# Graph network layers on one core: edges per node counted in the preparation, by ranks in the sorted destinations, and the preparation on tiles of 128 partitions

## The reference, cut to what matters

```python
def mesh_conv(x, src, dst, ea, w1, b1, g, bt, w2, b2):
    m = jnp.concatenate([x[dst], x[src], ea], axis=-1) @ w1 + b1
    m = jax.nn.silu(group_norm(m, g, bt))
    m = m @ w2 + b2
    n = x.shape[0]
    out = jax.ops.segment_sum(m, dst, num_segments=n)
    cnt = jax.ops.segment_sum(jnp.ones((dst.shape[0],), m.dtype), dst, num_segments=n)
    return out / jnp.clip(cnt, 1.0)[:, None]
# block 0: h = mesh_conv(...); norm, silu, + time embedding
#          h = mesh_conv(...) again; norm, silu, + x
#          attention over edges (8 heads, softmax per destination), output layer, norm
# block 1: graph attention (4 heads) over the same edges, with 128 edge features
```

## Time and profile before

| | us |
|---|---|
| median of 3 runs | 15801.92 (15791.97 to 15820.28) |
| span of the profiled execution | 12412.9 |
| median less span | 3389.0 |
| TensorE busy | 10184.1 (82% of the span) |
| VectorE busy | 6784.3 (55%) |
| GpSimd busy | 6565.9 (53%) |
| ScalarE busy | 4227.0 (34%) |

### The profile page before, as it was taken

One profiled execution on the slowest core, in us unless ns is written; L12 is line 12 of the kernel. 1 busy time (PEld: TensorE's weight loads), 2 busy tenths in 40 slices (PEclk: granted clock), 3 DMA queues, 4 the chain that ended last, 5 costly groups with the idle time before them and its releaser, 6 DMA issues. The chain is left out here.

```text
span 12412.9 us, 238807 instructions
## 1 busy us (share of the span) xinstructions
PE 10184.1 (82%) x52788; PEld 7837.8 (63%) x52788; DVE 6784.3 (55%) x13638; ACT 4227.0 (34%) x19321; POOL 6565.9 (53%) x6535
## 2 busy tenths in 40 slices
PE   0018999999999949999999569999996489999994
PEld 0015666666666637777777457777775378888882
DVE  0024555555555447777777546666665545555555
ACT  0003434433343404444344113333332045555552
POOL 0005444444444317777677237777774077777770
PEclk9996666666666658988898669999998589999996
DMA  1013222222222214444444246666663255555652
GB/s 17 14 48 88 83 82 83 82 82 82 82 84 81 65 58 118 123 121 121 116 121 119 72 118 178 180 178 178 180 178 106 57 130 134 136 136 134 134 135 74
DMA packets 1697918, 1336.67 MB, mean 108 GB/s; under 512 B 595131, under 2 KB 1473914, under 8 KB 1695443
## 3 DMA queue, kind: packets, MB, share of 16 engines
q1 hardware_dynamic: 1462376, 792.32, 23.6%
q0 software_dynamic: 234784, 537.91, 16.7%
HBM read 1255.24 MB, written 74.14 MB: 107 GB/s over the span
## 5 line engine op out<-in xcount | busy, mean ns | idle before, releaser
L452 POOL DMA_INDIRECT conv_gath<-b,conv_idx x3232 | 3262.3, 1009 | 3529.4 <-issue 1893.1
L830 POOL DMA_INDIRECT gat_gath<-g,gat_idx x1616 | 1606.2, 994 | 941.6 <-issue 495.5
L830 POOL DMA_INDIRECT attn_gath<-kv,attn_idx x1616 | 1642.8, 1017 | 847.0 <-issue 517.7
L476 PEld LDWEIGHTS conv_z<-conv_win,conv_hotT 128*128 128x128 f32 x6464 | 1226.0, 222 | 934.1 <-issue 705.0
L478 PE MATMUL conv_z<-wc,conv_ea 5*128 5x128 f32 x6464 | 1799.4, 363 | 0.0
L476 PE MATMUL conv_z<-conv_win,conv_hotT 128*128 128x128 f32 x6464 | 1719.6, 353 | 0.0
L594 DVE TENSOR_REDUCE conv_var<-conv_sq 128x32 f32<-128x512 f32 x808 | 551.7, 683 | 1891.1 <-ACT conv_sq L524 1891.0
L478 PEld LDWEIGHTS conv_z<-wc,conv_ea 5*128 5x128 f32 x6464 | 1100.8, 212 | 470.7 <-issue 173.1
L493 PE MATMUL conv_sums<-conv_hot,conv_m 128*128 128x128 f32 x6464 | 1319.2, 372 | 8.3 <-ACT conv_m L556 7.8
L493 PEld LDWEIGHTS conv_sums<-conv_hot,conv_m 128*128 128x128 f32 x6464 | 1138.8, 267 | 201.6 <-issue 167.5
L469 PE MATMUL conv_z<-conv_gath,ident 128*128 128x512 f32 x1616 | 1173.7, 818 | 58.8 <-DMA conv_gath<-b,conv_idx 58.7
(11 more groups left out here) (338 smaller groups left out, 17743.5 us busy)
## 6 DMA issues: line engine op xcount, KB each, us to landing
conv_win<-a SPq DMA_DIRECT2D x3232, 64.0 KB
conv_places<-places SPq DMA_DIRECT2D x202, 512.0 KB
attn_win<-q SPq DMA_DIRECT2D x1616, 64.0 KB
gat_xeT<-in_xeT SPq DMA_DIRECT2D x404, 256.0 KB
conv_gath<-b,conv_idx POOLq DMA_INDIRECT x3232
attn_places<-places SPq DMA_DIRECT2D x101, 512.0 KB
gat_places<-places SPq DMA_DIRECT2D x404, 128.0 KB
attn_gath<-kv,attn_idx POOLq DMA_INDIRECT x1616
```

The lines of the kernel that those rows point to most:

```text
L452: pool.indirect_dma_start(gath[:, b.c * BQ + k, t, :], None, b_table, bass.IndirectOffsetOnAxis(ap=idx[:, b.c, k * QT + t:k * QT + t + 1], ...
L476: nc.tensor.matmul(zt, hotT[:, s6, t * P:(t + 1) * P], win[:, s4, t, :], start=False, stop=False, skip_group_check=True)
L830: pool.indirect_dma_start(gath[:, b.c * BQ + k, t, :], None, table, bass.IndirectOffsetOnAxis(ap=idx[:, b.c, k * QT + t:k * QT + t + 1], a ...
```

## The change

1. The counts go out of `conv_edges`: `hot_b`, `counts`, the matmul with ones and the copies. `sums` has two buffers in both layers. The fold of layer 1 and the node stage "conv1" lose their part of it.
2. The preparation makes the counts. For each node it finds the number of edges whose destination is lower (its rank): first among the 101 first destinations of the batches (a comparison and a sum on VectorE), then among the 16 first destinations of the tiles of that batch, then among the 128 destinations of that tile. Between these, POOL gathers the rows that are needed, 49 indirect DMAs each time (one for each 128 nodes). Two small matmuls with a shift matrix subtract the rank of each node from that of the next.
3. The preparation works on 128 partitions: `cols` is now one table of [128, 2, 1616], `places` [128, 1664] and `mask` [1664, 129], each stored by one DMA; the mask's rows are no longer held eight times but are repeated when they are loaded. The loads of weights are shared between SP's and ScalarE's queues, and those of the edges come first, with a semaphore of their own.
4. The loads of `idx`, `cols`, `n0` and `mask` in the edge stages read from these new layouts.

The names `BT`, `BE` and `NB` of the batches are now `TB`, `EB` and `NBATCH`. The diff, cut:

```diff
-BT = 16
-BQ = BT // QT
-QE, BE = QT * P, BT * P
-NB = -(-E // BE)
-T = NB * BT
+TB = 16
+BQ = TB // QT
+QE, EB = QT * P, TB * P
+NBATCH = -(-E // EB)
+T = NBATCH * TB
 EP = T * P
-FR = -(-NP // NB)
+NB, BT, BE = 1, T, EP
+FR = -(-NP // NBATCH)
 RB = 3
-BODY = (NB - 2) // RB
-assert NBLK % GB == 0 and NGRP % 2 == 1 and BODY * RB + 2 == NB
+BODY = (NBATCH - 2) // RB
+assert NBLK % GB == 0 and NGRP % 2 == 1 and BODY * RB + 2 == NBATCH
 TC = -(-T // P)
 TP = TC * P
+TQ = TP // P
...
+        dst_c = st.sb("dst_c", [P, T], I32)
+        prev_c = st.sb("prev_c", [P, T], I32)
+        n0_all = st.sb("n0_all", [P, T], I32)
+        rel_c = st.sb("rel_c", [P, 2, T])
+
+        dst_q = st.sb("dst_q", [P, TQ * P], I32)
+        n0_q = st.sb("n0_q", [P, TQ], I32)
+        rel_q = st.sb("rel_q", [P, TQ * P], BF16)
+        mask = st.sb("mask", [P, TQ, P + 1])
...
+        below = st.sb("below", [P, NBLK, P])
+        n0_rows = st.sb("n0_rows", [P, NBLK, TB], I32)
+        dst_rows = st.sb("dst_rows", [P, NBLK, P], I32)
...
+        dst_pt = w["dst_b"].rearrange("o (p t) -> (o p) t", p=P)
+        FULL = (T // TQ) * P // P
+        edge_loads = [(n0_all[:, :], w["n0_p"][:, 0:T].to_broadcast([P, T])),
+                      (n0_q[:, :], w["n0_p"].rearrange("o (q t) -> (o q) t", t=TQ)),
+                      (dst_c[:, :], dst_pt), (prev_c[16:P, :], dst_pt[15:P - 1, :]),
+                      (prev_c[0:1, :], dst_pt[0:1, :]), (prev_c[1:16, :], dst_pt[0:15, :]),
+                      (dst_q[0:112, :], w["dst_r"][0, 0:112 * TQ * P].rearrange("(q e) -> q e", q=112)),
+                      (dst_q[112:FULL, :], w["dst_r"][0, 112 * TQ * P:FULL * TQ * P].rearrange("(q e) -> q e", q=FULL - 112))]
...
+            sp.wait_ge(padded, 1)
+            for dst, src in edge_loads:
+                sp.dma_start(dst, src).then_inc(edges_loaded, 16)
+            for dst, src in loads[0::2]:
...
-            sp.wait_ge(dve_made, 1)
-            sp.dma_start(D["cols"].rearrange("b p (a t) -> b a p t", a=2)[:, 0, :, :],
-                         rel_c[:, 0, :].rearrange("b (p t) -> b p t", t=BT)).then_inc(stored, 16)
-            sp.dma_start(D["cols"].rearrange("b p (a t) -> b a p t", a=2)[:, 1, :, :],
-                         rel_c[:, 1, :].rearrange("b (p t) -> b p t", t=BT)).then_inc(stored, 16)
-            sp.dma_start(D["places"], rel_h[:, :]).then_inc(stored, 16)
-            m = D["mask"].rearrange("(b t h) e -> b t h e", t=BT, h=NS)
-            for h in range(NS):
-                sp.dma_start(m[:, :, h, :], mask[:, :, :]).then_inc(stored, 16)
-            sp.wait_ge(stored, 16 * (4 + 3 + NS))
+            sp.wait_ge(cols_made, 1)
+            sp.dma_start(D["cols"], rel_c[:, :, :]).then_inc(stored, 16)
+            sp.wait_ge(places_made, 1)
+            sp.dma_start(D["places"], rel_q[:, :]).then_inc(stored, 16)
+            sp.wait_ge(mask_made, 1)
+            sp.dma_start(D["mask"].rearrange("(q t) e -> q t e", t=TQ), mask[:, :, :]).then_inc(stored, 16)
+            sp.wait_ge(stored, 16 * 7)
...
+            pool.wait_ge(batch_found, 1)
+            for b in range(NBLK):
+                pool.indirect_dma_start(n0_rows[:, b, :], None, w["n0_b"].rearrange("o (k t) -> (o k) t", t=TB),
+                                        bass.IndirectOffsetOnAxis(ap=batch_i[:, b:b + 1], axis=0)).then_inc(n0_gathered, 16)
+            pool.wait_ge(tile_found, 1)
+            for b in range(NBLK):
+                pool.indirect_dma_start(dst_rows[:, b, :], None, w["dst_r"].rearrange("o (t e) -> (o t) e", e=P),
+                                        bass.IndirectOffsetOnAxis(ap=tile_i[:, b:b + 1], axis=0)).then_inc(dst_gathered, 16)
+            pool.wait_ge(dst_gathered, NBLK * 16)
...
+            for dst, src in loads[1::2]:
+                act.dma_start(dst, src).then_inc(loaded, 16)
...
+            pe.wait_ge(ranked, 1)
+            nc.tensor.matmul(p_n[:, 0:2 * NBLK], shift[:, :], tile[:, :, 0:NBLK], start=True, stop=False)
+            nc.tensor.matmul(p_n[:, 0:2 * NBLK], corner[:, :], tile[:, :, 1:NBLK + 1], start=False, stop=True)\
+              .then_inc(degree_ready, 1)
...
+            nc.vector.memset(dst_q[:, :], N).then_inc(padded, 1)
...
+            dve.wait_ge(edges_loaded, EDGE_LOADS)
+            link(nc.vector.tensor_copy(n0_f[:, :], n0_all[:, :].rearrange("p (k t) -> p k t", t=TB)[:, :, 0]))
+            link(nc.vector.tensor_tensor(below[:, :, 0:NBATCH], bc(n0_f[:, :].unsqueeze(1), wide),
+                                         bc(node[:, :].unsqueeze(2), wide), ALU.is_lt))
+            link(nc.vector.tensor_reduce(batch[:, :], below[:, :, 0:NBATCH], AX.X, ALU.add))
+            link(nc.vector.tensor_scalar(batch[:, :], batch[:, :], -1.0, 0.0, ALU.add, ALU.max))
+            link(nc.vector.tensor_copy(batch_i[:, :], batch[:, :]))
+            dve.sem_inc(batch_found, 1)
+
+
+            link(nc.vector.tensor_tensor(rel_c[:, 0, :], dst_c[:, :], n0_all[:, :], ALU.subtract))
+            link(nc.vector.tensor_tensor(rel_c[:, 1, :], dst_c[:, :], prev_c[:, :], ALU.not_equal))
+            link(nc.vector.memset(rel_c[0:1, 1, :], 1.0))
+            dve.sem_inc(cols_made, 1)
+            rel_t = rel_q[:, :].rearrange("q (t e) -> q t e", e=P)
+            link(nc.vector.tensor_tensor(rel_t, dst_q[:, :].rearrange("q (t e) -> q t e", e=P),
+                                         bc(n0_q[:, :].unsqueeze(2), [P, TQ, P]), ALU.subtract))
+            dve.sem_inc(places_made, 1)
             link(nc.vector.memset(mask[:, :, :], -BIG))
             link(nc.vector.tensor_tensor(mask[:, :, 1:P], rel_t[:, :, 1:P], rel_t[:, :, 0:P - 1], ALU.not_equal))
             link(nc.vector.tensor_scalar(mask[:, :, 1:P], mask[:, :, 1:P], -BIG, None, ALU.mult))
-            dve.sem_inc(dve_made, 1)
-
+            dve.sem_inc(mask_made, 1)
...
+            dve.wait_ge(n0_gathered, NBLK * 16)
+            wide = [P, NBLK, TB]
+            link(nc.vector.tensor_tensor(below[:, :, 0:TB], n0_rows[:, :, :], bc(node[:, :].unsqueeze(2), wide), ALU.is_lt))
+            link(nc.vector.tensor_reduce(tile[:, 0, 0:NBLK], below[:, :, 0:TB], AX.X, ALU.add))
+            link(nc.vector.scalar_tensor_tensor(tile[:, 0, 0:NBLK], batch[:, :], float(TB), tile[:, 0, 0:NBLK], ALU.mult, ALU.add))
+            link(nc.vector.tensor_scalar(tile[:, 0, 0:NBLK], tile[:, 0, 0:NBLK], -1.0, 0.0, ALU.add, ALU.max))
+            link(nc.vector.tensor_copy(tile_i[:, :], tile[:, 0, 0:NBLK]))
+            dve.sem_inc(tile_found, 1)
+
+
+            dve.wait_ge(dst_gathered, NBLK * 16)
+            wide = [P, NBLK, P]
+            link(nc.vector.tensor_tensor(below[:, :, :], dst_rows[:, :, :], bc(node[:, :].unsqueeze(2), wide), ALU.is_lt))
+            link(nc.vector.tensor_reduce(tile[:, 1, 0:NBLK], below[:, :, :], AX.X, ALU.add))
+            dve.sem_inc(ranked, 1)
+
+
+            dve.wait_ge(degree_ready, 1)
+            link(nc.vector.tensor_copy(degree[:, :], p_n[:, NBLK:2 * NBLK]))
+            link(nc.vector.scalar_tensor_tensor(degree[:, :], p_n[:, 0:NBLK], float(P), degree[:, :], ALU.mult, ALU.add))
+            link(nc.vector.tensor_scalar(cnt[:, 0, :], degree[:, :], 1.0, None, ALU.max))
+            link(nc.vector.reciprocal(cnt[:, 0, :], cnt[:, 0, :]))
+            link(nc.vector.tensor_scalar(cnt[:, 1, :], degree[:, :], 0.0, 1.0, ALU.max, ALU.min))
...
+    return D["places"].rearrange("q e -> (q e)")[bass.ds(e, n)].unsqueeze(0).to_broadcast([P, n])
...
+    ZQ, SQ = 6, 2
...
-                for dst, src in ((idx[:, b.c, :], w["src_b"][bass.ds(b.i, 1), :, :].rearrange("a p t -> (a p) t")),
-                                 (places[:, b.c, :], D["places"][bass.ds(b.i, 1), :].to_broadcast([P, BE])),
-                                 (cols[:, b.c, :], D["cols"][bass.ds(b.i, 1), :, :].rearrange("a p t -> (a p) t")),
-                                 (ea[:, b.c, :], w["ea"][:, bass.ds(b.i * BE, BE)]),
-                                 (n0[:, b.c, :], w["n0_b"][bass.ds(b.i, 1), :])):
+                for dst, src in ((idx[:, b.c, :], w["src_b"][0, :, bass.ds(b.i * TB, TB)]),
+                                 (places[:, b.c, :], places_of(D, b.i * EB, EB)),
+                                 (cols[:, b.c, :].rearrange("p (a t) -> p a t", a=2), D["cols"][:, :, bass.ds(b.i * TB, TB)]),
+                                 (ea[:, b.c, :], w["ea"][:, bass.ds(b.i * EB, EB)]),
+                                 (n0[:, b.c, :], w["n0_b"][:, bass.ds(b.i * TB, TB)])):
...
-                if l == 1:
-                    done(pe, counts_freed, g)
-                    done(pe, hot_b_ready, g + 1)
-                    nc.tensor.matmul(counts[0:1, :], C["ones_b"][:, :], hot_b[:, k % 2, :], start=True, stop=True)\
-                      .then_inc(counts_ready, 1)
...
-                outs = [(count, first_count, counts[0:1, :], counts_ready, counts_copied, counts_freed)] if l == 1 else []
-                outs.append((acc, first, sums[so][:, :], sums_ready, sums_copied, sums_freed))
```

(35 more changed lines are left out.)

200 lines of the change are left out of this document (98 added, 102 removed).

## The result

| | us | range |
|---|---|---|
| before | 15797.19 | 15791.97 to 15820.28, 4 runs |
| after | 14713.01 | 14705.99 to 14714.28, 4 runs |
| ratio | 0.9302 | 95% interval 0.9286 to 0.9319 |

The change makes the kernel 7.0% faster, 1084 us. 14112 us (10.7%) were forecast, and the range ended at 14500 us, so size and range were wrong and the sign was right. The profiled execution of the changed kernel took 14714.28 us and has a span of 14712.5 us: nothing lies outside of the span. The 3389 us of the kernel before therefore needed another explanation, and the first experiment looks for it.

The account below looks back on a forecast made before the run. TensorE, busy 82% of the 12412.9 us span, was taken as the bound, with the preparation waiting for DMAs. Gains of 1051 + 626 + 5 + 8 = 1690 us took 15802 to 14112 us; range 13600 to 14500 us.

Parts of the forecast that it names:

- The 3389 us: Timed median 15801.92 less profiled span 12412.9 us; the forecast supposed that this rest outside the span stays.
- layer 1's 1051 us: Convolution layer 1 falls from 3399.3 to layer 2's 2348.0 us, as its program becomes that of layer 2.
- the path through the clock: Layer 1: some 640 of TensorE's 853 us busy-time fall come from remaining matmuls running at a higher clock.
- Rival A: Layer 1 keeps its clock and gains some 420 us instead of 1051; time 14743 us; chance 7%.
- the direct part: Layer 1: TensorE loses 211 us of count matmuls and 205 us of idle time before them, some 420 us.
- The mark that I set for A: Layer 1 at 2950 us with a clock of 0.66 would show that it keeps its clock.
- The copies of counts: Layer 1: ScalarE's 412 us of copies lie in the chain ending TensorE's idle time; not counted a second time.
- Rival C: The 3389 us are slower execution of the same work; gain grows by 1.27 to 2150 us, time 13650; chance 15%.
- The preparation: First stage ends at about 196 us instead of 822.5, a gain of 626 us; ends 150 and 330 us.
- Rival D: Preparation's gathers queue at 5.33 us each, 549 us for 98; preparation 600 us, time 14520 us; chance 4%.
- Small parts: Fold of layer 1 gains 5 us, node stage "conv1" 8 us (ends 0 and 16).
- The sum: 1051 + 626 + 5 + 8 = 1690 us off span and median: span 10723 us, time 14112 us.

Follow-up runs that it names:

- the first experiment: The kernel before, unchanged, profiled a second time: 15685.92 us, ratio 1.001, profiled span 15686.8 us.
- e11: The changed kernel, unedited, on a chip where the kernel before took 12508.35 us: 10795.61 us, ratio 0.8639.
- e1: The kernel before, unchanged, run for a second profile: 15685.92 us against 15666.93 us, ratio 1.001.
- e2: The kernel before without counts (reciprocals set to one, division left out), with two buffers of sums in both layers, old preparation and layouts: 15163.95 us, ratio 0.9687.
- e5: The kernel before without counts, with one buffer of sums in both layers: 13096.88 us against 12500.67 us, ratio 1.0484.
- e10: The changed kernel with one buffer of sums instead of two in both convolution layers: 15362.57 us, ratio 0.9699 to the kernel before.
- e6: The kernel before without ScalarE's copies of the counts, cast and count matmul kept: 12353.54 us, ratio 0.9889.
- e3: The changed kernel with `cols` and `idx` stored and read batch by batch as before: 14572.59 us, ratio 0.9309 to the kernel before.
- e4: The changed kernel with all loads of the preparation on SP's queue, none on ScalarE's: 14592.83 us, ratio 0.9322 to the kernel before.

## Why the prediction was wrong, by its steps

**The steps that failed: layer 1's 1051 us taken over to the timed executions, and with it the supposition that the 3389 us stay.** As a statement on the quick trace, the difference of two stages, it was right: e11 takes 1013 us off layer 1 (3399.3 - 2386.1), and the span of 10758.5 us is within 0.4% of the forecast 10723. With it the path through the clock was given too much: TensorE's busy time falls by 812 us between before and e11 (3169 to 2358), near the 853 us that the prediction has, but by 336 us between e1 and the result (3234 to 2898). The time to be forecast was of executions in which layer 2 itself takes 3283 us (e1). There the gain of layer 1 is 508 us (e2 against e1) or 459 us (the result against e1). The excess over the quick kind, supposed to stay, grew from 3274 us before to 3954 us after (14712.5 - 10758.5), in layer 1 above all: from 396 to 950 us. The stage was slow before through its own single buffer; once that is gone it is as slow as layer 2 there, for a reason that stays open.

**Rival A came out by its number, and only in part by its mechanism.** It had 7%: the layer keeps its clock and gives back the direct part only, 420 us, time 14743 us. Measured were 14713 us, a clock of 0.65 before and 0.69 after, and 459 to 508 us. But two of its terms were not what they seemed. The 205 us of idle time were put down to the counts, and in e5 and e10 they stand there without counts (193 and 307 us). And with the counts out and one buffer, TensorE is busy as long as in e1 (3235 us in e10, 3234 in e1): the 211 us of count matmuls came back as slower matmuls at a clock of 0.60. The second buffer then took off 351 us of busy time. That the sum of the two steps lies near 420 us is luck. The mark that I set for A, 2950 us, is missed because it was counted from the quick 3399. The mistake is in the weighing: "layer 2 runs high after equal starts" was read from an execution that was not one of those timed.

**The copies of counts.** The prediction has them in the chain that ends the idle time before the count matmul. The row itself names "issue" for 186 of the 205 us, and e6 took the copies away and gained 56 us. What made the other matmuls slow was the single buffer of sums (e5), a part of the change that the prediction has as a detail of the counting.

**Rival C had the right premise and the wrong arithmetic.** The 3389 us were slower execution of the same work. But the gain does not grow by 1.27 with the time; it shrinks, since the preparation takes 822 us on either kind of chip (DMAs at 16 GB/s) and layer 1 was slow already. That the missing time could be slower execution deserved more than multiplying all by one factor: stage by stage it must lie where the clock was high, in layer 2 too, and then layer 1 cannot come down to 2348 us.

**The preparation: right.** Forecast 196 us, measured 182.8; -640 us instead of -626. The edge loads ended at 20.3 us instead of 28. The gathers took 1051 ns each in the first round and 946 in the second, 49 x 105 ns = 5.1 us more, where 5 was taken for VectorE beside them. The excess lies in four gathers of 1.40 to 2.65 us at 32 to 44 us, while VectorE makes the tables; no run takes VectorE away. The largest operations took 5.3 and 6.7 us as computed. The stores are hidden. The busy shares of the DMA engines and what they moved in the stage, in 40 slices of 4.6 us, show it:

```profile
DMA  3999952066611111111111011111211111110000
GB/s 99 343 253 217 174 105 56 2 227 250 183 6 8 7 6 7 7 6 7 7 6 6 14 50 50 57 49 51 57 46 55 57 43 57 57 43 14 0 0 0
```

The three slices of 227, 250 and 183 GB/s at 37 to 50 us are the stores of `cols`, `places` and `mask`, in some 14 us where 28 had been estimated, and 184 at 16 GB/s. The stores of before, of `cols` and then of `mask`:

```profile
105.00:256.00 151.00, 2.48 (x11) 2.17 (x11) 10.38 (x41) 0.00 (x0) 0.00 (x0) 1.00 0.12 5
408.00:820.00 412.00, 0.00 (x0) 0.00 (x0) 0.00 (x0) 0.00 (x0) 0.00 (x0) 1.00 0.07 17
```

The Trainium skill (DMA: Bandwidth & Descriptors, "Why a DMA increments its semaphore by 16 and not by 1") lets one DMA of 128 rows be shared out over 16 engines and one of 101 rows over a single one; these rows agree: the share is 0.6 now and was 0.07, about one engine of 16, while `mask` was stored (0.12 with the two stores of `cols`). But the number of rows is not all that changed. The bytes fell from 8.7 to 2.9 MB, and `cols`, which went out in pieces of 64 bytes at 5 GB/s and not at 17, now goes out in long rows. No run holds these apart. Rival D falls: only four gathers were over 1 us.

**Small parts: right.** The fold of layer 1 takes 37.4 instead of 42.1 us; the node stage "conv1" 194.4 instead of 205.7 us (e1), -11 where -8 was taken.

**The sum.** On the slow chips 640 + 459 + 5 + 11 = 1115 us, or 1164 with e2's 508, against 1084 us measured. The rest is within what the unchanged stages vary between executions: layer 2 takes 3283, 3293 and 3334 us in e1, e2 and the result.

**Open.** Why TensorE pauses on a slow chip, and what would cure it, is not shown. No experiment on half of the gathers or windows came to such a chip, so only the place of the pauses is known, not their cause. Nor is it shown why one timing on a quick chip took 16,482 us. None of e3, e4 and e10, which compute the same as the changed kernel, has a ratio below its 0.9302.

## What to carry to other kernels

Before a stage of the trace is priced, hold the span of the profiled execution against the time of the runs. Where they differ by much, ask which stages can hold the difference; a gain that comes through a higher clock counts only if the timed executions grant that clock to like stages. Give the direct part (instructions and the waits before them) and the part through the clock as two terms, with a chance for each. When two things change at once, as counts and buffer did here, price each by a run of its own before the sum is trusted: a wait that stands before an instruction need not be that instruction's. And look at a stage in which every engine and the DMAs are idle first: the preparation, 5% of the time before, gave 640 of 1084 us.

## What the runs showed of the hardware that was not expected

- The same program on one core takes 12,508 us on one chip and 15,840 us on another (before), and 10,796 and 14,751 us (after). VectorE is busy as long (6784 and 6759 us in before), and so are ScalarE (4227 and 4231 us) and the preparation with its slow DMAs (822 us); TensorE's clock is 0.86 in a layer on the one and 0.69 on the other, between its two levels of 1.2 and 2.4 GHz.
- 104 waits of at most 2.0 us, 190 us in a layer of 3196 us, went with a clock of 0.66 (e5), where without them it was 0.86 (e11). Layer 2, where before and e5 differ in the buffer alone, shows the same: 2348 us at 0.88 and 3235.5 us at 0.65.
- A second PSUM buffer of sums was worth 810 us of 3196 where the clock rose from 0.66 to 0.86, and 297 of 3640 where it rose from 0.60 to 0.69 only.
